# First attention without the twelve unread TensorE products that stand inside its head pairs

## The chip, the cores and the metric

The kernel runs on one core of a Trainium2 chip. The metric is the device time of one execution in microseconds; before the change the median of three runs is 1009.01 us (1003.79 to 1011.23). A core has five engines that run their own instruction streams and meet at semaphores: PE (TensorE, matrix products and transposes into PSUM), DVE (VectorE), ACT (ScalarE), POOL (GpSimd) and SP (SyncE, which here issues DMAs). TensorE's clock is granted at one of two levels, 2.4 GHz (shown as 1.00) or 1.2 GHz (0.50).

## The reference, cut to what matters

The input is `x` of 4 batch entries, 512 rows and 256 columns, in f32. Four layers follow, each with a residual and a layer norm:

- a causal softmax attention with 16 heads of 16 columns, rotary angles on the first 4 of them (the first attention);
- a gated wave layer with two levels of linear maps and norms;
- a linear attention;
- six MLP blocks with 1024 hidden columns.

```
qkv = einsum('bsh,hf->bsf', x, w_qkv) + b_qkv          # split in 16 heads, q and k rotated
scores = where(causal, einsum('bhqd,bhkd->bhqk', q, k), -inf)
attn = einsum('bhqk,bhkd->bhqd', softmax(scores), v)
x = layernorm(x + attn @ w_out + b_out)
```

The products that the change leaves out compute nothing of this: their results are never read.

## The kernel before, in words

f32 operands are split into a high and a low part (names with `_h` and `_l`), and a product is made of three.

**First attention** (function `attention0`, the four batch entries are "entries"). An entry works through 8 pairs of heads `p`, and a pair through 4 steps `r` (row tiles). In each step TensorE makes two score products (L858), two products for the row maximum of the pair two ahead (L847), a share of the value products of earlier pairs (L871), and, where a table (`WORK_AT`, `FIRST_AT`, `LAST_AT`) has an entry for the step `(p, r)`, one piece of other work (`use_work`): a projection of q, k and v (L894), a turn of the stacked heads by transposes (`turn_stack`, L901; the k half into the bank `work`, the q half into the bank `exchange`), a transpose of the next entry's `x` (`x_T`, L978), an output projection (L910), or work on later layers' weights (L935, L946, L957, L964). `work` and `exchange` are one PSUM bank each: a piece may start only when the engine that reads the piece before has counted up `work_read` or `ex_read`. An entry is "first" (entry 0), "loop" (1 and 2) or "last" (3). The order on every engine is written out by the program; nothing is reordered at run time but by these waits.

Readers: DVE finds the maxima (L1148), makes the low part of the transposed `x` (`x_l`, L1185) and adds the bias to a projection (L1197); ACT does the exponentials (L722), copies the turned heads (L709, L715), makes the high part of the transposed `x` (`x_h`, L690) and stacks heads (L701, L703); POOL masks the diagonal (L606), rotates (L591 to L595) and makes the low half of the stacks (L612, L614).

**Unread products.** `keep_busy` (L985) issues products of 128 by 128 with 512 columns of `wout_h` into a bank whose content nobody reads. It is called in three places:

- before the entries, while the second pair's maxima are made: 4, 3, 2 and 2 products (L1078);
- in `use_work` (L917 to L920), in step (0, 2) of the first entry and the two loop entries, ahead of the turn of the stack (1, 1): 3 products into `exchange` each, behind a wait until the q copy of the stack before is done;
- in `entry` (L1016 to L1019) by the table `KEEP_AT` (L316), in step (6, 2) of the first entry: 3 products into `work`, behind a wait until DVE has added the bias of the projection just made.

Ahead of the turn of a stack stand further waits: that DVE has read the transposed `x` out of `work`, and that POOL has made the stack's low half (L921, L925).

Of the kernel before, what the change touches and what calls it, by code (L numbers as in the profile page):

```python
# [194 lines left out]
def sems(stack, nc, names, of=""):  # L195
    return {n: stack.enter_context(nc.semaphore(of + n)) for n in names.split()}


def build(nc, A, out):
# [3 lines left out]
    with top:  # L203
# [109 lines left out]
BIAS_TILE_AT = ((5, 1), (5, 2), (5, 3), (6, 0))  # L313
KEEP_TILE_AT = ((6, 2), (6, 3), (7, 0), (7, 1))

KEEP_AT = {"first": {(6, 2): (3, ("project", (3, 2)))},  # L316
           "loop": {}, "last": {}}


def of_entry(when, half):  # L320
# [3 lines left out]
def work_table(when):  # L324

    table = {}
    for p, r, kind, arg in WORK_AT:
        if kind in PREVIOUS:
            used = when != "first"
        else:  # L330
            used = when != "last" if kind == "x_T" else of_entry(when, arg[0])
        if used:
            table[p, r] = (kind, arg)
    for p, r, kind, arg in {"first": FIRST_AT, "loop": (), "last": LAST_AT}[when]:
        table[p, r] = (kind, arg)
    return dict(sorted(table.items()))
# [39 lines left out]
WORK = Uses([], lambda when: list(work_table(when).values()), [])  # L376
EXCHANGE = Uses([("neg", 0)], exchange_list, [("group", -1)])


def attention0(nc, A, g, top):  # L380
# [21 lines left out]
    s = g.first = sems(top, nc, "ident_in rope_in const_in first_T first_p first_v first_s first_copied qkv_in0 qkv_in1 out_in wsplit_h wsplit_l g_wout const_v mask_v x_in xres_in g_res g_ones "  # L402
             "p_work work_read p_ex ex_read a_xT a_attT a_nT v_xT g_rope g_chain g_val a_stack stack_low "
             "p_max v_max v_neg m_row0 m_row1 p_score a_exp g_sel p_out a_out v_chain v_norm g_x1 "
             "phase_in v_turn a_sin v_mod mod_out mod_in small_in wave_rows_in path_in gate_in ent_in l1_in last_in "
             "v_bias v_matrix a_split v_split a_gate_h v_gate_l p_gate a_gate p_tail v_tail a_c")
# [29 lines left out]
    def stage_matrix(st):  # L436
        return entangled[:, MATRIX_AT[st] // 2, :, :] if MATRIX_AT[st] % 2 else raw_path[:, MATRIX_AT[st], :, :]
# [22 lines left out]
    work, outputs, exchange = ps[:, 5, :], ps[:, 6, :], ps[:, 7, :]  # L460
    block = g.block = top.enter_context(nc.Block())

    def tile_number(i, half, t):

        return RT * (2 * i + half) + t
# [17 lines left out]
    def wait(eng, sem, count):  # L483

        if not isinstance(count, int) or count > 0:
            eng.wait_ge(sem, count)
# [343 lines left out]
    def _(pe):  # L830
# [83 lines left out]

        def use_work(i, when, kind, arg):

            if (kind, arg) == ("stack", (1, 1)) and when != "last":  # L917

                pe.wait_ge(s["ex_read"], EXCHANGE.number(i, when, (kind, arg)))
                keep_busy(exchange, 3)  # L920
            wait(pe, s["work_read"], WORK.number(i, when, (kind, arg)))  # L921
            if kind == "project":
                mm = project(work, *arg)
            elif kind == "stack":
                pe.wait_ge(s["stack_low"], tile_number(i, *arg) + 1)  # L925
                mm = turn_stack(work, k_stack)
            elif kind == "out":
                mm = project_out(work, arg)
            elif kind == "bias":
                pe.wait_ge(s["small_in"], 96 + 16 * 2 * (STAGES - 1))  # L930
                mm = pe.transpose(work[:, 0:BIAS_COLS], bias_rows[:, :], ident[0:BIAS_COLS, 0:BIAS_COLS])
            elif kind == "total":
                pe.wait_ge(g.wave["v_turns"], 3)
                pe.wait_ge(s["work_read"], WORK.number(i, when, ("constant", arg)) + 1)
                mm = pe.matmul(work[:, 0:D], g.turns[:, 2:3].broadcast_to([P, P]), g.stage_c[:, 2 * arg + 1, :],  # L935
                               start=True, stop=True)
            elif kind == "constant":
                if arg:
                    pe.wait_ge(s["ent_in"], 32 * MC0)
                else:  # L940
                    pe.wait_ge(g.pre["w1_in"], 16)
                pe.wait_ge(s["v_bias"], 1)
                for m in range(MC0):
                    rows = slice(m % 4 * GROUP_ROWS, (m % 4 + 1) * GROUP_ROWS)
                    col = 4 + arg * MC0 + m
                    mm = pe.matmul(work[rows, 0:D], g.bias_col[:, col:col + 1].broadcast_to([P, GROUP_ROWS]),  # L946
                                   raw_pw[:, m, :], start=(m < 4), stop=(m >= MC0 - 4))
            elif kind == "entangle":
                l, part = arg[0], arg[-1]
                if l:  # L950
                    pe.wait_ge(s["ent_in"], 32 * MC0)
                else:
                    pe.wait_ge(g.pre["w1_in"], 16)
                    pe.wait_ge(g.pre["w2_in"], 16)
                for n in range(MC_HALF):
                    m = part * MC_HALF + n
                    mm = pe.matmul(work[:, 0:D], ent_t[:, m, arg[1] * P:(arg[1] + 1) * P], raw_pw[:, m, :],  # L957
                                   start=(n == 0), stop=(n == MC_HALF - 1))
            elif kind == "offset":

                pe.wait_ge(s["v_matrix"], MATRIX_NUMBER[arg])
                for c in range(KC):
                    col = SB_COL + (arg - 1) * KC + c
                    mm = pe.matmul(work[:, 0:D], g.bias_col[:, col:col + 1].broadcast_to([P, P]),  # L964
                                   stage_matrix(arg)[:, c, :], start=(c == 0), stop=(c == KC - 1))
            else:
                if kind == "x_T":
                    pe.wait_ge(s["x_in"], 16 * (i + 2))
                    src = x_in
                elif kind == "att_T":  # L970

                    pe.wait_ge(s["ex_read"], EXCHANGE.number(i, when, ("group", -1)) + 1)
                    src = att
                else:
                    pe.wait_ge(s["v_norm"], i + 1)
                    src = xn[:, 0, :, :]
                for t in range(RT):
                    mm = pe.transpose(work[:, t * P:(t + 1) * P], src[:, t, arg * P:(arg + 1) * P], ident[:, :])  # L978
            mm.then_inc(s["p_work"], 1)
            if kind == "stack":  # L980
                pe.wait_ge(s["ex_read"], EXCHANGE.number(i, when, (kind, arg)))
                mm = turn_stack(exchange, q_stack)
                mm.then_inc(s["p_ex"], 1)

        def keep_busy(bank, count):  # L985
            for _ in range(count):
                pe.matmul(bank, wout_h[:, 0, 0:P], wout_h[:, :, :].rearrange("p c d -> p (c d)"), start=True, stop=True)

        def entry(i, when):
            table = work_table(when)  # L990
            for p in range(PAIRS):
                for r in range(RT):
                    if (i, p, r) != (0, 0, 0):
                        score_pass(i, p, r)
                    if p + 2 < PAIRS:
                        max_pass(i, p + 2, r, (i, when))
                    elif when != "last":
                        max_pass(i + 1, p + 2 - PAIRS, r, (i, when))

                    if p % 2 and r >= 2:  # L1000
                        value_pass(i, p // 2, r - 2)
                    elif p % 2 == 0 and r < 2 and p:
                        value_pass(i, p // 2 - 1, r + 2)
                    elif p == 0 and r < 2 and when != "first":
                        value_pass(i - 1, GROUPS - 1, r + 2)
                    row_next = r == 1 and (p < PAIRS - 1 or when != "last")

                    if row_next and p != 1:
                        max_rows(i, when, p + 1, i * PAIRS + p + 1)
                    if (p, r) in table:  # L1010
                        use_work(i, when, *table[p, r])
                    if row_next and p == 1:
                        max_rows(i, when, p + 1, i * PAIRS + p + 1)
                    if group_at(p, r, when):
                        transpose_outputs(i, when, p // 2 - 1)
                    if (p, r) in KEEP_AT[when]:  # L1016
                        count, use = KEEP_AT[when][p, r]
                        wait(pe, s["work_read"], WORK.number(i, when, use))
                        keep_busy(work, count)  # L1019

        def first_project(half, t, bank):
            project(ps[:, bank, :], half, t).then_inc(s["first_p"], 1)
# [1839 lines left out]
```

## Time and profile before

| what | value |
|---|---|
| median of three runs | 1009.01 us (1003.79 to 1011.23) |
| the profiled execution: its own time | 1004.3 us |
| the profiled execution: span of the profile | 1002.3 us |
| mean granted clock of TensorE over the span | 0.996 |
| busy, share of the span: PE, DVE, ACT, POOL | 96%, 76%, 61%, 36% |

The span runs from the first to the last instruction; 2.0 us of the profiled execution's time lie around it. A busy time is the union of an engine's instructions. PE's includes the way of a product through the pipeline, so neighbouring products overlap and a fully busy PE need not be at its peak. The idle time in brackets behind a row of the timeline is the engine's, just before that row, with what ended it.

### The profile page before, as it was taken

To read this page: it belongs to the slowest core of one execution; us is meant where nothing else is said; L and a number is where in the kernel's file an instruction comes from. 1 tells how busy PE (TensorE), PEld (TensorE's weight loads), DVE (VectorE), ACT (ScalarE), POOL (GpSimd) and SP (SyncE) were. 2 spreads that over 40 slices of the span, in tenths; PEclk is the share of its full clock that TensorE was granted. 3 is DMA by queue.
4 is the path that set the end of the run, shared out by engine and by line. 5 is a ranking of instruction groups with operands and counts; after the bars stand their busy time and mean duration, and the time that the engine had idled before them with its cause. 6 is when DMAs were issued, how large, how long until landed. Compare 5 with 4: busy or idle time off the path is not lost.

```text
span 1002.3 us, 18316 instructions
## 1 busy us (share of the span) xinstructions
PE 960.4 (96%) x6487; PEld 797.8 (80%) x6487; DVE 758.4 (76%) x2090; ACT 609.2 (61%) x1177; POOL 360.6 (36%) x646
## 2 busy tenths in 40 slices
PE   8899999999899898889999999999999999999997
PEld 7565565656468897778899999999999999999897
DVE  6677787877948779867658787876878787687874
ACT  6456767656479674455546666655666655566650
POOL 4445466473221674343822222322222232222410
PEclk9899999999999999999999999999999999999999
DMA  7100011101120000022202120221212022121211
GB/s 254 32 1 23 23 33 43 43 23 55 59 54 4 1 22 23 19 88 64 84 12 63 33 64 22 64 66 31 64 31 63 23 64 67 31 62 32 63 37 50
DMA packets 55043, 47.42 MB, mean 47 GB/s; under 512 B 7108, under 2 KB 52392, under 8 KB 54952
## 3 DMA queue, kind: packets, MB, share of 16 engines
q1 hardware_dynamic: 52632, 43.75, 14.5%
q10 hardware_dynamic: 2320, 2.49, 0.8%
q8 instruction: 52, 0.85, 0.3%
q14 instruction: 39, 0.32, 0.1%
HBM read 31.40 MB, written 4.20 MB: 36 GB/s over the span
## 4 chain that ended last, share of the span: by engine, by line
PE 54%; DVE 5%; POOL 2%; issue 1%; ACT 1%; DVEq 0%; POOLq 0%; ACTq 0%
PE ps L2000 25%; PE ps L2017 24%; PE ps L1898 2%; DVE ln_stats L2418 1%; PE ps L2030 1%; PE ps L1949 1%; POOL hs L1795 1%; DVE xT_l L2552 0%; POOL x_b L1795 0%; PE ps L1912 0%; DVE amp L2454 0%; PE ps L1927 0%; DVE G_l L2558 0%; PE ps L1940 0%; PE ps L1849 0%
## 5 line engine op out<-in xcount | busy, mean ns | idle before, releaser
L2254 ACT ACTIVATE G<-ps,bias_col 128x512 f32<-128x512 f32 x192 | 135.8, 707 | 156.5 <-PE ps L2000 148.1
L2017 PE MATMUL ps<-w_l,G_h 128*128 128x256 f32 x736 | 203.8, 277 | 0.0
L2017 PE MATMUL ps<-w_h,G_l 128*128 128x256 f32 x736 | 203.8, 277 | 0.0
L2017 PE MATMUL ps<-w_h,G_h 128*128 128x256 f32 x736 | 203.7, 277 | 0.0
L2558 DVE TENSOR_TENSOR G_l<-G,G_h 128x512 fp32r<-128x512 f32 x192 | 166.3, 867 | 48.3 <-ACT G_h L2255 48.3
L1825 POOL TENSOR_TENSOR x_a<-xn,mlp_g 128x1024 f32<-128x1024 f32 x20 | 56.1, 2803 | 326.6 <-DVE xn L2584 326.6
L2000 PE MATMUL ps<-xT_h,w_h 128*128 128x512 f32 x384 | 150.3, 391 | 0.6 <-DVE xT_l L2552 0.4
L722 ACT ACTIVATE probs<-ps 128x512 f32<-128x512 f32 (+3 forms) x256 | 98.4, 441 | 85.4 <-PE ps L858 84.8
L2000 PE MATMUL ps<-xT_h,w_l 128*128 128x512 f32 x384 | 149.7, 390 | 0.0
L2000 PE MATMUL ps<-xT_l,w_h 128*128 128x512 f32 x384 | 149.5, 389 | 0.0
L2017 PEld LDWEIGHTS ps<-w_h,G_h 128*128 128x128 f32 x736 | 138.4, 188 | 0.9
L2017 PEld LDWEIGHTS ps<-w_l,G_h 128*128 128x128 f32 x736 | 138.2, 188 | 1.0
L2017 PEld LDWEIGHTS ps<-w_h,G_l 128*128 128x128 f32 x736 | 138.2, 188 | 0.0
L1148 DVE CUSTOM_DVE_ANT_0 ps<-ps,q_mask 128x128 f32<-128x128 f32 (+3 forms) x256 | 120.8, 513 | 21.0 <-PE ps L847 20.0
L2255 ACT ACTIVATE G_h<-ps,bias_col 128x512 fp32r<-128x512 f32 x192 | 135.3, 705 | 0.0
L606 POOL TENSOR_SCALAR_AFFINE_SELECT probs<-probs 128x256 f32<-128x256 f32 x128 | 52.9, 414 | 87.8 <-ACT probs L722 87.0
L2000 PEld LDWEIGHTS ps<-xT_h,w_h 128*128 128x128 f32 x384 | 72.1, 188 | 15.3 <-issue 0.6
L2000 PEld LDWEIGHTS ps<-xT_h,w_l 128*128 128x128 f32 x384 | 72.1, 188 | 15.2
L2000 PEld LDWEIGHTS ps<-xT_l,w_h 128*128 128x128 f32 x384 | 72.1, 188 | 14.0
L2572 DVE TENSOR_TENSOR rsum<-ps,x_a 128x1024 f32<-128x1024 f32 x23 | 28.2, 1225 | 68.3 <-PE ps L2017 68.3
L847 PE MATMUL ps<-heads_T 64*128 64x128 f32 (+3 forms) x256 | 56.9, 351 | 7.1 <-DVE top_score L1148 6.9
L858 PE MATMUL ps<-heads_T 64*128 64x512 f32 (+3 forms) x256 | 53.4, 413 | 2.9 <-ACT probs L722 2.2
(333 smaller groups left out, 2081.6 us busy)
## 6 DMA issues: line engine op xcount, KB each, us to landing
w_raw<-L_ffn_W_T SPq DMA_DIRECT2D x12, 1024.0 KB, 5.4
landed<-squares SPq DMA_DIRECT2D x320, 32.0 KB, 1.9
hs<-L_attn_hidden_states SPq DMA_DIRECT2D x8, 512.0 KB, 3.9
x_kept<-hs SPq DMA_DIRECT2D x4, 512.0 KB, 3.3
w_raw<-x_kept SPq DMA_DIRECT2D x2, 1024.0 KB, 5.5
out<-xn SPq DMA_DIRECT2D x3, 512.0 KB, 2.8
w_raw<-L_ffn_ent_w_T SPq DMA_DIRECT2D x1, 1024.0 KB, 9.4
w_raw<-L_ffn_ent_pw SPq DMA_DIRECT2D x1, 1024.0 KB, 11.6
```

Of the source, the lines that this page charges most:

```text
L606: pool.affine_select(diagonal, diagonal, [[0, 2], [1, P]], ALU.is_ge, 0.0, base=0, channel_multiplier=-1).then_inc(s["g_sel"], 1)
L722: act.activation(probs[:, p % 2, o, OFF[j]:OFF[j] + COLS[j]], ps[:, score_bank(r, o), 0:COLS[j]], ACT.Exp).then_inc(s["a_exp"], 1)
L847: pe.matmul(ps[:, o, 0:(t + 1) * P], heads_T[rows, p // UP, 0, p % UP, t * P:(t + 1) * P], heads_T[rows, p // UP, 1, p % UP, 0:(t + 1) * P ...
L858: pe.matmul(ps[:, score_bank(r, o), 0:COLS[j]], heads_T[rows, p // UP, 1, p % UP, j * P:(j + 1) * P], heads_T[rows, p // UP, 0, p % UP, j ...
L1148: v.tensor_tensor_reduce(ps[:, o, 0:(t + 1) * P], ps[:, o, 0:(t + 1) * P], q_mask[:, S - (t + 1) * P:S], 1.0, MASKED, ALU.add, ALU.max, to ...
L1825: pool.tensor_tensor(g.x_a[:, rows, :], xn[:, b % 2, :, :], bcast(g.mlp_g[:, i, :], 1, [P, RT, D]), ALU.mult).then_inc(feed["g_mul"], 1)
L2000: mm = pe.matmul(ps[:, hidden_bank(i, n), :], w[:, c, f * P:(f + 1) * P], x[:, b, c, :], start=(k == 0), stop=(k == 5))
L2017: mm = pe.matmul(ps[:, 4 + t // 2, (t % 2) * D:(t % 2 + 1) * D], x[b % 2][f][:, t * P:(t + 1) * P], w2_chunk(w, f), start=(k == 0), stop=( ...
L2254: act.activation(G32[n % 4], bank, ACT.Gelu, bias=bias)
L2255: act.activation(G_h[b % 2][f], bank, ACT.Gelu, bias=bias).then_inc(feed["a_g"], 1)
L2558: v.tensor_tensor(G_l[b % 2][f], G32[n % 4], G_h[b % 2][f].bitcast(F32), ALU.subtract).then_inc(feed["v_gl"], 1)
L2572: v.tensor_tensor(g.rsum[:, :, :], ps[:, 4:6, :].rearrange("p a (b c) -> p (a b) c", c=D), g.x_a[:, b * RT:(b + 1) * RT, :], ALU.add).then ...
```

## The change: the edit

The wait and the three products at the head of `use_work` go, and with them the table `KEEP_AT` and its use at the end of a step. These are 3 products in each of the first entry and the two loop entries at step (0, 2), and 3 in the first entry at step (6, 2): twelve of the 23 that `keep_busy` makes. The eleven before the entries stay.

```
-KEEP_AT = {"first": {(6, 2): (3, ("project", (3, 2)))},
-           "loop": {}, "last": {}}
...
         def use_work(i, when, kind, arg):
 
-            if (kind, arg) == ("stack", (1, 1)) and when != "last":
-
-                pe.wait_ge(s["ex_read"], EXCHANGE.number(i, when, (kind, arg)))
-                keep_busy(exchange, 3)
             wait(pe, s["work_read"], WORK.number(i, when, (kind, arg)))
...
                     if group_at(p, r, when):
                         transpose_outputs(i, when, p // 2 - 1)
-                    if (p, r) in KEEP_AT[when]:
-                        count, use = KEEP_AT[when][p, r]
-                        wait(pe, s["work_read"], WORK.number(i, when, use))
-                        keep_busy(work, count)
```

The wait that goes with the products of step (0, 2) is made again a few instructions later, ahead of the q half of the same turn (L981).

## Rows read from the trace of the kernel before

**Rows 1.** Page, busy us of the engines (share of the span) and instructions
```profile
PE 960.4 (96%) x6487; PEld 797.8 (80%) x6487; DVE 758.4 (76%) x2090; ACT 609.2 (61%) x1177; POOL 360.6 (36%) x646
```

**Rows 2.** Windows, entry 1: length, then PE, PEld, DVE, ACT, POOL busy, clock, DMA
```profile
97.17:160.23 63.06, 59.29 (x446) 37.14 (x443) 49.93 (x190) 41.57 (x106) 34.91 (x96) 1.00 0.12 36
```

**Rows 3.** Line L987, the unread products: ns min/median/max, first and last start
```profile
L987 PE MATMUL ps<-wout_h x23: 388/397/792, 24.1 to 164.8; 128*128 128x512 f32 x23
```

**Rows 4.** Timeline of PE, step (0, 2) of entries 1 and 2: start, us, work
```profile
101.15 0.96 PE L987 MATMUL ps<-wout_h 128*128 128x512 f32 x3
102.08 0.53 PE L901 MATMUL ps<-ident_r,k_stack 128*128 128x128 f32 x4
...
103.88 0.63 PE L887 MATMUL ps<-ident,out_T 128*128 128x128 f32 x4 [0.26 <-ACT heads_T L715]
105.03 0.50 PE L858 MATMUL ps<-heads_T 64*128 64x512 f32 x2 [0.53 <-ACT probs L722]
...
164.19 0.97 PE L987 MATMUL ps<-wout_h 128*128 128x512 f32 x3
165.13 0.54 PE L901 MATMUL ps<-ident_r,k_stack 128*128 128x128 f32 x4
```

**Rows 5.** Timeline of DVE, low part of the transposed x, entries 0, 1, 2
```profile
36.27 0.69 DVE L1185 TENSOR_TENSOR x_l<-ps,x_h 128x512 fp32r<-128x512 f32 x1 [0.90 <-ACT x_h L690]
...
101.33 0.69 DVE L1185 TENSOR_TENSOR x_l<-ps,x_h 128x512 fp32r<-128x512 f32 x1 [0.83 <-ACT x_h L690]
...
164.38 0.69 DVE L1185 TENSOR_TENSOR x_l<-ps,x_h 128x512 fp32r<-128x512 f32 x1 [0.83 <-ACT x_h L690]
```

**Rows 6.** Waits from 100 to 103: who for whom, us, times, longest
```profile
PEld ps L901 <- DVE x_l L1185: 0.4, 1, 0.4
```

**Rows 7.** Timeline of PE, step (6, 2) of the first entry and behind
```profile
87.31 0.98 PE L987 MATMUL ps<-wout_h 128*128 128x512 f32 x3
88.21 0.39 PE L858 MATMUL ps<-heads_T 64*128 64x256 f32 x2
...
90.33 0.32 PE L847 MATMUL ps<-heads_T 64*128 64x128 f32 x1 [0.33 <-DVE top_score L1148]
```

**Rows 8.** Timelines of ACT and DVE over the same steps
```profile
87.06 0.88 ACT L722 ACTIVATE probs<-ps 128x384 f32<-128x384 f32 x2 [1.99 <-PE ps L858]
...
88.87 0.70 DVE L1148 CUSTOM_DVE_ANT_0 ps<-ps,q_mask 128x512 f32<-128x512 f32 x1 [0.49 <-PE ps L847]
```

**Rows 9.** Timelines of PE and ACT, pair 0 of the first entry
```profile
31.40 1.03 PE L847 MATMUL ps<-heads_T 64*128 64x128 f32 x2 [0.94 <-DVE top_score L1148]
...
36.47 1.60 PE L987 MATMUL ps<-wout_h 128*128 128x512 f32 x3
37.91 0.47 PE L901 MATMUL ps<-ident_r,k_stack 128*128 128x128 f32 x4
...
39.20 1.99 PE L957 MATMUL ps<-w_raw 128*128 128x256 f32 x8
...
38.41 0.60 ACT L709 ACTIVATE heads_T<-ps 128x512 fp32r<-128x512 f32 x1 [1.28 <-PE ps L901]
```

**Rows 10.** Windows of the low clock, and of the same work in two entries
```profile
31.06:37.89 6.83, 6.32 (x26) 4.53 (x27) 4.30 (x20) 3.52 (x9) 1.64 (x4) 0.50 0.02 4
...
98.11:103.61 5.50, 5.50 (x48) 3.64 (x44) 2.93 (x12) 5.18 (x13) 2.49 (x7) 1.00 0.12 39
32.36:39.27 6.91, 6.86 (x38) 5.00 (x37) 4.23 (x14) 4.37 (x11) 1.64 (x4) 0.60 0.01 2
```

**Rows 11.** Timeline of PE, value products that only entry 1 has there
```profile
99.34 0.64 PE L871 MATMUL ps<-probs,val 128*32 128x256 f32 x8
```

**Rows 12.** Windows with idle TensorE: ahead of the low clock, and elsewhere
```profile
28.87:31.40 2.53, 1.59 (x7) 0.70 (x7) 1.43 (x6) 1.09 (x2) 0.43 (x2) 0.93 0.73 207
101.22:105.03 3.81, 3.02 (x19) 2.01 (x20) 3.24 (x10) 3.58 (x10) 1.48 (x5) 1.00 0.20 70
...
444.00:447.40 3.40, 1.78 (x12) 1.14 (x11) 3.30 (x13) 1.92 (x6) 1.48 (x2) 1.00 0.01 2
```

## The prediction

> **What bounds the kernel now.** The page comes first: TensorE is busy for 960.4 of 1002.3 us [rows 1], so time is won or lost there. The change sits in the first attention, so I cut that into entries: entry 1 takes 63.06 us, of which TensorE is busy for 59.29 and the next engine, DVE, for 49.93 [rows 2]. TensorE is the bound on average, but with 3.8 us of idle time, so an instruction less on it returns its time only where nothing else is late at that place. The line of the unread products gives their number, 23, and a median of 397 ns each [rows 3]; eleven of them stand before the entries and stay. The timelines show the twelve others as four bursts, which I call A (36.47, first entry), B (87.31, first entry), C (101.15, entry 1) and D (164.19, entry 2) [rows 4, 7, 9]. At each the question is what TensorE would do instead, and that is read from who ends the next wait. The granted clock is the second half of the question: it is at its high level all through the entries but for one stretch of 6.83 us, from 31.06 to 37.89, where it is 0.50, which is 1.2 instead of 2.4 GHz [rows 10].
>
> **C and D return nothing.** The next work is the turn of a stack, and it needs the bank that still holds the transposed `x`, until DVE has taken its low part. DVE starts that at 101.33 and takes 0.69 us, so it ends at 102.02; the turn starts at 102.08 [rows 4, 5]. At D it ends at 164.38 + 0.69 = 165.07 and the turn starts at 165.13 [rows 4, 5]. The same 0.06 us both times is how a release looks, and the weight load of the turn is indeed put down to `x_l` [rows 6]. DVE itself waits for ACT, which the products do not hold up. So the 0.96 and 0.97 us are laid over a wait that stays: 0 each, and TensorE then stands idle from about 101.22 to 102.08. What covers the edit here is DVE's wait; only if the transposed `x` came earlier would there be something to gain, at most the 0.9 us of a burst.
>
> **B returns about 0.5 us.** The products run from 87.31 to the next score product at 88.21. That one needs the first of the two exponentials that ACT makes from 87.06 in 0.88 us, so about 87.5 [rows 7, 8]: TensorE can be 0.65 us earlier. DVE stands idle for 0.49 us before the maximum that follows and is what TensorE waits for next, at 90.33 [rows 7, 8]. It can be early by those 0.49 us and not more, since before them it is at work. I take 0.5; the ends are 0 and the whole burst, 0.98.
>
> **A returns about 0.6 us.** Here the clock is low and the burst takes 1.60 us. The low part of `x` is there at 36.27 + 0.69 = 36.96, so the turn could start at 37.02 instead of 37.91: 0.89 us at most [rows 5, 9]. What follows is late for another reason: the work at 39.20 needs the bank that ACT copies from 38.41 to 39.01 [rows 9], and the turn ahead of that copy would now run at the low clock throughout. A half of it is there within 0.53 us at the high clock [rows 4] and takes longer at the low one, so I set 0.3 us against the 0.89 for both halves and take 0.6, which I chose. The ends are 0 and 0.89.
>
> The removed wait on `ex_read` costs nothing and gives nothing: it is made again ahead of the q half. No transfer, queue or operation of another engine moves; twelve weight loads go with the products.
>
> So without any effect on the clock the sum is -0.6 - 0.5 - 0 - 0 = **-1.1 us**, with ends of 0 and -0.89 - 0.98 - 0.9 - 0.9 = -3.7. The profiled execution would go from 1004.3 to 1003.2 us. It is 4.7 us under the median of the runs shown, so I carry differences over to the median: 1009.0 - 1.1 = 1007.9.
>
> **What a fall of the clock costs.** The change puts idle time into TensorE where products stood. What does the trace show of that? Ahead of the one fall TensorE was busy for 1.59 us of 2.53, with a longest gap of 0.94 us [rows 9, 12]. From 101.22 to 105.03 it is now busy for 3.02 of 3.81, and without the burst it would lose another 0.86 of that, with gaps of 0.86, 0.26 and 0.53 us [rows 4, 12]. That looks like the place of the fall. On the other side, from 444.00 to 447.40 TensorE is busy for 1.78 of 3.40 us and the clock stays at 1.00 [rows 12]. So such a gap allows a fall and does not force one, and I can only set odds: about one in three each at C and D, less at B, where the next work closes up by 0.65 of the burst's 0.98 us, and one in four at A that the clock rises later than at 37.89, since the burst fills the end of the low stretch.
>
> The price comes from the same work at both levels. From the first turn of pair 0 to the end of the maxima of step 2, entry 1 takes 5.50 us, of which 0.64 are value products that the first entry has not yet; that leaves 4.86. The first entry takes 6.91, mostly at the low clock [rows 10, 11]. So a fall costs 6.91 - 4.86 = **2.0 us**. The ends are 0, if TensorE would have waited anyway, and half of the 6.83 us, 3.4, if it did nothing but products.
>
> The Trainium skill, page "TensorE: Matmul & The Clock Gate", section "A second HAM failure mode: psum-queue depth-cycling", speaks against the change: a kernel whose TensorE idles briefly but often between groups of products can go back and forth between the two levels of the clock. By it each new gap would bring a fall. The trace agrees for the one fall at 31.06 and disagrees for 444.00 to 447.40 [rows 12], so it gets a chance and not the forecast.
>
> **The rivals.**
> Forecast: one more fall in the typical execution, from the odds above (two thirds for C and D together, about a third for A and B). -1.1 + 2.0 = +0.9, so 1009.9. Chance 0.42.
>
> No fall, only the cover is gone: 1007.9. For it speaks that the clock holds through the idle stretch at 444.00, against it that it fell once with gaps of the same length. Chance 0.28.
>
> Slower: the clock falls in the gap at the head of the entries each time, at C and D, and rises later at A. Three prices of 2.0 less the 0.5 of B: +5.5, so 1014.5. The mechanism decides where the gap ahead of the turn of stack (1, 1), the rest being the short transposes and half-height products around it, is enough by itself to bring the low level. For it speaks the match with the stretch before 31.06, against it that the trace has as idle a stretch without a fall. To be slower than 1% (10.1 us) it needs falls of 3.4 us, at which it is 3 x 3.4 - 0.5 = 9.7 and the gaps of later steps join in. Chance 0.20, of which 0.08 over 1%.
>
> Faster: the bursts are on the path after all, and the time of all four returns: 1.60 + 0.98 + 0.96 + 0.97 = 4.5 us [rows 4, 7, 9], so 1004.5. For it speaks only TensorE's busy share in entry 1; against it the equal 0.06 us at C and D. Chance 0.07.
>
> That the change does not do what it says can be all but excluded: the products have a line of their own, and 11 of 23 should be left on it. The remaining 0.03 is for a median that comes out low for no reason of the change.
>
> **How the numbers follow.** Likeliest is 1010. About 1% is what a measurement of this kernel can tell from no change, since the three runs shown lie 7.4 us apart. All cases but the far end of the slower one lie inside: within 1% 0.89, slower 0.08, faster 0.03. The range reaches from the full return, a little under 1004.5, to a little over the slower case of 1014.5: 1003.5 to 1015.
>
> **What the profile after would show.** Line L987's place has 11 products, none after 30 us. In pair 0 of entries 1 and 2 the turn starts 0.06 us after `x_l` as now, behind an idle gap of some 0.85 us put down to DVE. Behind step (6, 2) of the first entry DVE's idle time of 0.49 us is gone. The row of the granted clock tells the rest: entries 1 and 2 at 1.00 throughout mean no fall there, and a mean below 1.00 in either is one. The prediction is wrong if the turn at C or D starts well before 102.02's counterpart, if a fall costs far from 2.0 us in the same work, or if the clock is unchanged and the time yet moves by more than the bursts' 4.5 us.

## The result and the profile after

The changed kernel takes 1010.75 us in the median of 20 runs (1009.50 to 1014.73), the kernel before, beside it, 1006.30 (20 runs, 1003.41 to 1011.23). The ratio is 1.0041, 95% interval 1.0027 to 1.0054: by the ratio 4.1 us slower, within 1%. The profiled execution took 1012.74 us, 2.0 over the median; TensorE makes 6475 products in it, twelve fewer than in [rows 1].

First the clock. The windows of the changed kernel (columns as in [rows 2]) are entry 1, entry 2, and then the five stretches at the low level inside the first attention:

```profile
97.82:160.75 62.93, 58.29 (x443) 36.59 (x440) 49.88 (x190) 41.55 (x106) 34.81 (x96) 1.00 0.11 36
160.75:225.50 64.75, 60.85 (x444) 38.06 (x440) 50.04 (x190) 41.63 (x106) 34.80 (x96) 0.95 0.10 31
...
31.00:41.24 10.24, 9.24 (x40) 6.82 (x41) 6.92 (x24) 5.77 (x15) 3.33 (x9) 0.50 0.02 8
167.53:174.36 6.83, 6.71 (x37) 4.30 (x37) 4.30 (x19) 5.19 (x15) 3.55 (x11) 0.50 0.04 13
252.87:256.28 3.41, 3.41 (x20) 2.79 (x23) 3.26 (x13) 0.45 (x2) 0.66 (x2) 0.50 0.00 0
266.52:280.17 13.65, 13.50 (x42) 7.45 (x42) 10.30 (x42) 5.16 (x13) 3.11 (x6) 0.50 0.32 83
287.00:293.83 6.83, 6.20 (x32) 2.60 (x36) 2.71 (x5) 3.66 (x9) 3.90 (x8) 0.50 0.54 168
```

Where the kernel before has one low stretch of 6.83 us [rows 10], this has 41.0 us in five. The profiled execution before was one with little of it, at a mean clock of 0.996; the means over many runs, further down, lie closer together. Entry 1, which answers to [rows 2], is no longer than before (62.93 against 63.06) at a clock of 1.00: C's removal alone moved nothing.

The timeline of TensorE at C and D answers to [rows 4]; its lines are numbered lower in the changed kernel (L900 is the turn, L886 the transposes of the outputs, L846 and L857 the products for maxima and scores):

```profile
101.52 0.34 PE L846 MATMUL ps<-heads_T 64*128 64x384 f32 x2
102.72 0.54 PE L900 MATMUL ps<-ident_r,k_stack 128*128 128x128 f32 x4 [0.86 <-DVE x_l L1176]
...
104.53 0.63 PE L886 MATMUL ps<-ident,out_T 128*128 128x128 f32 x4 [0.27 <-ACT heads_T L714]
105.69 0.50 PE L857 MATMUL ps<-heads_T 64*128 64x512 f32 x2 [0.53 <-ACT probs L721]
```
```profile
165.65 0.54 PE L900 MATMUL ps<-ident_r,k_stack 128*128 128x128 f32 x4 [0.87 <-DVE x_l L1176]
...
167.46 1.04 PE L886 MATMUL ps<-ident,out_T 128*128 128x128 f32 x4 [0.27 <-ACT heads_T L714]
168.62 0.79 PE L857 MATMUL ps<-heads_T 64*128 64x512 f32 x2
```

The turn waits 0.86 us for `x_l` at C and 0.87 us at D. At C the steps then run as before; at D, with the same steps and the same gaps, the clock falls while the transposes of the outputs run, and they take 1.04 us instead of 0.63.

The low part of `x` that the turn waits for answers to [rows 5]:

```profile
101.98 0.69 DVE L1176 TENSOR_TENSOR x_l<-ps,x_h 128x512 fp32r<-128x512 f32 x1 [0.83 <-ACT x_h L689]
...
164.91 0.69 DVE L1176 TENSOR_TENSOR x_l<-ps,x_h 128x512 fp32r<-128x512 f32 x1 [0.83 <-ACT x_h L689]
```

101.98 + 0.69 = 102.67 and 164.91 + 0.69 = 165.60: the turns follow 0.05 us later.

TensorE at B, which answers to [rows 7], and at A, which answers to [rows 9]:

```profile
88.59 0.39 PE L857 MATMUL ps<-heads_T 64*128 64x256 f32 x2 [0.40 <-ACT probs L721]
89.00 0.93 PE L846 MATMUL ps<-heads_T 64*128 64x512 f32 x2
...
90.77 0.51 PE L846 MATMUL ps<-heads_T 64*128 64x128 f32 x2
```
```profile
36.98 0.75 PE L900 MATMUL ps<-ident_r,k_stack 128*128 128x128 f32 x4 [0.48 <-DVE x_l L1176]
...
39.10 3.03 PE L952 MATMUL ps<-w_raw 128*128 128x256 f32 x8
42.06 0.51 PE L857 MATMUL ps<-heads_T 64*128 64x512 f32 x2
```

At A the turn starts at 36.98 instead of 37.91, but the clock stays low until 41.24, and the eight products behind take 3.03 us where they took 1.99.

Set against the same instruction in the kernel before, the lag of the changed kernel's TensorE is +0.95 us behind A, +0.64 behind B, +0.65 behind C, +2.3 behind D, and +8.5 at the end of the attention; from there to the end of the kernel it no longer changes. The lag is the difference of the start times in the two profiles. So 6 us of the profiled execution's loss lie in the last entry, from which nothing was removed.

### The profile page after: what moved, and what is told of

Its sections match the earlier page's. It is cut to its first block, busy times and chain, and to the rows that moved or that the text cites. A ratio compares the mean times of both kernels' runs of the same rounds, so it can differ in the third digit from the quotient of the medians.

```text
span 1010.7 us, 18292 instructions
## 1 busy us (share of the span) xinstructions
PE 969.3 (96%) x6475; PEld 802.7 (79%) x6475; DVE 759.0 (75%) x2090; ACT 609.1 (60%) x1177; POOL 360.9 (36%) x646
## 4 chain that ended last, share of the span: by engine, by line
PE 54%; DVE 5%; POOL 2%; issue 1%; ACT 1%; DVEq 0%; POOLq 0%; ACTq 0%
PE ps L1991 24%; PE ps L2008 24%; PE ps L1889 2%; DVE ln_stats L2409 1%; PE ps L2021 1%; PE ps L1940 1%; POOL hs L1786 1%; DVE xT_l L2543 0%; POOL x_b L1786 0%; PE ps L1903 0%; DVE amp L2445 0%; PE ps L1918 0%; DVE G_l L2549 0%; PE ps L1931 0%; PE ps L1840 0%
## 5 line engine op out<-in xcount | busy, mean ns | idle before, releaser
L846 PE MATMUL ps<-heads_T 64*128 64x128 f32 (+3 forms) x256 | 57.7, 362 | 5.0 <-DVE top_score L1139 4.8
L857 PE MATMUL ps<-heads_T 64*128 64x512 f32 (+3 forms) x256 | 56.2, 435 | 3.1 <-ACT probs L721 2.3
## 6 DMA issues: line engine op xcount, KB each, us to landing
w_raw<-L_ffn_ent_w_T SPq DMA_DIRECT2D x1, 1024.0 KB, 10.2
```

The costliest lines, as they stand in the source:

```text
L846: pe.matmul(ps[:, o, 0:(t + 1) * P], heads_T[rows, p // UP, 0, p % UP, t * P:(t + 1) * P], heads_T[rows, p // UP, 1, p % UP, 0:(t + 1) * P ...
L857: pe.matmul(ps[:, score_bank(r, o), 0:COLS[j]], heads_T[rows, p // UP, 1, p % UP, j * P:(j + 1) * P], heads_T[rows, p // UP, 0, p % UP, j ...
```

## The experiments

Two theories stood after the result. **Theory 1**: the low stretches depend on when an idle stretch of the attention meets the clock's changes, so moving work moves them. **Theory 2**: they come at the place of the removed burst, and the last entry's are chance. The expectations were written with these names.

The table gives all runs; low time, the time at the low clock, is 2 x (1 - mean granted clock) x time, the mean over a kernel's runs. In the profiles 1.3 to 3.7 us of it lie at the end of the span, and in two of them 3.4 us near 450 us; all else lies in the attention. For the kernel before it is 18.9, 21.2 and 19.3 us in the three sets of 28 to 35 runs beside these, for the changed kernel 36.6. The changed kernel was run in the first set only; the later kernels are compared with it by their ratios and low time.

| kernel | median us (runs) | ratio to before, 95% | low time us |
|---|---|---|---|
| changed | 1010.75 (20) | 1.0041 (1.0027 to 1.0054) | 36.6 |
| before_shift10 | 1011.75 (7) | 1.0051 (1.0026 to 1.0077) | 27.2 |
| after_shift5 | 1008.80 (10) | 1.0016 (0.9997 to 1.0035) | 22.4 |
| after_last | 1008.65 (10) | 1.0020 (1.0000 to 1.0040) | 23.6 |
| before_last | 1006.67 (10) | 1.0003 (0.9982 to 1.0025) | 12.9 |
| only_A | 1010.62 (12) | 1.0032 (1.0012 to 1.0053) | 30.8 |
| only_CD | 1008.79 (12) | 1.0013 (0.9993 to 1.0033) | 25.9 |
| only_B | 1010.73 (12) | 1.0043 (1.0021 to 1.0064) | 32.4 |
| filled | 1006.51 (12) | 0.9981 (0.9961 to 1.0000) | 11.7 |
| after_filled | 1009.18 (12) | 1.0028 (1.0010 to 1.0046) | 22.9 |
| fill_early | 1005.61 (12) | 0.9977 (0.9962 to 0.9992) | 14.2 |
| fill_early_noB | 1005.52 (12) | 0.9977 (0.9955 to 0.9999) | 13.1 |
| filled2 | 1007.20 (12) | 0.9999 (0.9981 to 1.0018) | 10.9 |

**The price of low time** is read from the runs of the kernel before. In each of the three sets time follows the mean clock with a correlation of 0.98; in the last, the two fastest runs (1003.0 and 1003.1 us) have 0.997 and 0.998, the two slowest (1011.1 and 1011.3 us) 0.984. The slopes of the three sets (574, 614 and 571 us for a clock of 1) make 0.28 to 0.30 us for each us at the low clock (574 / 2 / 1007 is 0.285); 0.29 is used below. This is a mean price over all places, and a correlation: the traces show that it differs by place. The lag grows by 1.8 us over the 6.83 us at D (0.26 for each us), and in before_last's profile by 1.5 us over the 3.41 us at 145 us (0.44), where the other engines have less to do.

**before_shift10: later work, nothing removed.**

```
                         transpose_outputs(i, when, p // 2 - 1)
+                    if (i, p, r) == (2, 7, 2):
+                        pe.wait_ge(s["ex_read"], EXCHANGE.number(i, when, ("neg", PAIRS)) + 1)
+                        keep_busy(exchange, 10)
```

> The kernel before with ten more unread products at step (7, 2) of entry 2, where TensorE has no idle time: all twelve bursts stay, and everything behind is 10 x 0.21 = 2.1 us later, about as late as the changed kernel's last entry is (+2.2 us). Theory 1 (the low stretches of the last entry come from when its idle stretches fall, not from what was removed): the clock falls in the last entry as in the changed kernel's profile (three stretches there, 23.9 us in all at 0.50), so +2.1 and a further 4 to 6 us against before, ratio 1.006 to 1.008. Theory 2 (low stretches come only where a burst was taken away; the last entry's are chance): +2.1 us, ratio 1.002, with the last entry at its clock of before.

Ratio 1.0051, 5.1 us, where the ten added products make the lag grow by 2.3 in the profile (2.1 was reckoned). Most of the rest goes with low time, 27.2 us against 18.9: 8.3 x 0.29 = 2.4. Its profile has a stretch in the last entry, and two more in entries that are instruction for instruction those of the kernel before:

```profile
144.66:148.07 3.41, 3.41 (x17) 1.74 (x17) 0.74 (x5) 2.04 (x4) 0.41 (x1) 0.50 0.00 0
209.51:212.92 3.41, 3.41 (x17) 1.85 (x16) 0.61 (x4) 1.56 (x4) 0.41 (x1) 0.50 0.00 0
270.95:281.19 10.24, 10.09 (x36) 5.51 (x33) 8.64 (x35) 5.16 (x13) 3.12 (x6) 0.50 0.37 104
```

The profile of before_last has the same two. So the kernel before, which is the same program up to there, falls at 145 and 210 us too, in some executions and not in the one of [rows 10]. Theory 2's 1.002 lies outside the interval; theory 1's 1.006 to 1.008 lies above the ratio measured, its lower part still inside the interval, and its three stretches in the last entry were one, of 10.24 us.

**after_shift5: the changed kernel with more work** (the same edit on the changed kernel, with a count of 5).

> The changed kernel with five unread products at step (7, 2) of entry 2: 1.1 us more work on TensorE, none of the twelve back. Theory 1: the last entry is moved by 1.1 us to another place against the clock's changes, so its low stretches are others than the three of the changed kernel; less low time there, and the time falls below the changed kernel's although work was added (by 2 to 5 us). Theory 2: 1.1 us slower than the changed kernel, ratio to before 1.005.

Theory 1 fits and theory 2 does not: 1.1 us of added work, and 2.5 us less by the ratios (1.0041 to 1.0016); theory 2's 1.005 lies outside the interval. The two intervals overlap, but low time says the same, 22.4 us against 36.6: the ten runs have 18 to 32 us, the twenty of the changed kernel 30 to 49. In the profile the first stretch is at another place and shorter, ahead of the added work, and the last entry has one of 3.41 us:

```profile
33.75:40.58 6.83, 6.36 (x26) 4.60 (x27) 4.73 (x13) 4.45 (x13) 3.35 (x9) 0.50 0.01 2
...
286.34:289.75 3.41, 3.41 (x30) 1.22 (x26) 0.55 (x1) 1.25 (x4) 1.71 (x4) 0.50 0.46 190
```

**after_last and before_last: cover in the last entry.**

```
-           "loop": {}, "last": {}}
+           "loop": {}, "last": {(4, 1): (3, ("offset", 1)), (5, 1): (3, ("offset", 2)), (6, 0): (3, ("next_T", 0)), (6, 3): (3, ("next_T", 1)), (7, 0): (3, ("next_T", 1))}}
```

This is the edit of before_last. after_last puts the same table, with an empty "first", and its use at the end of a step into the changed kernel.

> The changed kernel with 15 unread products in idle stretches of the last entry (3 each at the end of steps (4, 1), (5, 1), (6, 0), (6, 3) and (7, 0)), none of the twelve back. If low stretches of the last entry make most of the loss (theory 1), the clock stays at 1.00 there from step (4, 1) on and 3 to 5 us come back: ratio to before 0.999 to 1.002. If the loss lies at the places of the removed bursts (theory 2), nothing comes back: ratio 1.004 or above, by up to 15 x 0.2 = 3 us of added work.

> The kernel before with the same 15 unread products in the last entry, its own 23 kept. If the last entry of the kernel before is now and then low as well (its runs lie up to 8 us apart), its median falls by 1 to 3 us and its runs lie closer together (ratio 0.997 to 0.999); if its last entry is always at 1.00, it is 0 to 3 us slower by the added work (ratio 1.000 to 1.003).

On the changed kernel half of the loss returns by the ratios (1.0020), and its ten runs have 20 to 26 us of low time, where the changed kernel's have 30 to 49. Its profile has no low stretch behind 256.19, while those at 30.91 to 41.15 and 167.44 to 174.27 are where they were:

```profile
252.78:256.19 3.41, 3.41 (x21) 2.85 (x23) 3.22 (x13) 0.45 (x2) 0.61 (x2) 0.50 0.00 0
265.00:300.00 35.00, 32.78 (x195) 19.24 (x194) 19.96 (x71) 20.66 (x46) 11.52 (x22) 1.00 0.25 80
```

On the kernel before (1.0003, and not the 0.997 to 0.999 of the first case) low time falls by 6.0 us, and the added products take back what that gives.

**only_A, only_CD, only_B: which burst matters.** The changed kernel with one kind of burst back:

```
         def use_work(i, when, kind, arg):
+            if (kind, arg) == ("stack", (1, 1)) and when == "first":
+
+                pe.wait_ge(s["ex_read"], EXCHANGE.number(i, when, (kind, arg)))
+                keep_busy(exchange, 3)
```

This is only_A; only_CD has `"loop"` in place of `"first"`, and only_B puts back the table `KEEP_AT` and its use instead.

> The changed kernel with burst A alone back (three products at step (0, 2) of the first entry). Theory 1 (time = a part without low clock, 1.2 us less than before, plus 0.29 us for each us at the low clock): A shortens the first low stretch from 10.2 to 6.8 us, 1.0 us, and costs at most the 0.6 us that its removal was to give; the low stretch near 167 us stays. So 0.4 to 1.0 us less than the changed kernel: ratio to before 1.003. Theory 2 (what matters is the place of each burst alone, and A's is the whole loss): ratio 1.000.

> The changed kernel with bursts C and D alone back (three products at step (0, 2) of both loop entries). By the prediction they cost nothing, being laid over a wait, and D keeps the clock up near 167 us, where the three profiles without it fall for 6.8 us: 2.0 us less than the changed kernel, ratio to before 1.002; mean clock 0.985 against 0.982. If the fall there had another cause, no difference to the changed kernel: 1.004.

> The changed kernel with burst B alone back (three products at step (6, 2) of the first entry). The profiles show no low stretch at B in any kernel without it, and 0.33 us given back there. So B does nothing for the clock and costs 0.3 us: mean clock 0.982 as in the changed kernel, ratio to before 1.004 to 1.005. If B kept the clock up in executions that no profile showed, the mean clock is 0.984 or more and the ratio 1.003 or less.

By the ratios C and D are worth 2.8 us of the 4.1, A 0.9 and B nothing. The three ratios are in or near what was expected (only_CD has less than its 1.002, inside the interval). Only only_B's mean clock, 0.984 where 0.982 was expected, speaks for B, and its ratio does not. The intervals of only_A and only_CD both reach into that of the changed kernel, so this rests as much on the windows of their profiles. For each of only_A, only_CD and only_B, the first stretch and the place of D (for only_B, between them, that of B):

```profile
31.21:38.04 6.83, 6.54 (x28) 4.72 (x29) 4.30 (x18) 3.52 (x9) 1.64 (x4) 0.50 0.01 2
160.00:175.00 15.00, 13.00 (x111) 8.05 (x111) 10.91 (x44) 12.15 (x31) 8.38 (x25) 1.00 0.16 54
```
```profile
31.82:42.06 10.24, 9.45 (x42) 6.98 (x42) 6.29 (x22) 5.77 (x15) 3.34 (x9) 0.50 0.01 1
...
160.00:175.00 15.00, 13.87 (x113) 8.63 (x115) 10.80 (x42) 12.26 (x32) 9.09 (x25) 1.00 0.19 54
```
```profile
31.90:42.14 10.24, 9.45 (x41) 6.93 (x41) 6.35 (x22) 5.77 (x15) 3.34 (x9) 0.50 0.01 1
84.00:94.00 10.00, 9.60 (x63) 6.14 (x55) 6.71 (x27) 4.83 (x14) 3.96 (x13) 1.00 0.00 0
168.43:175.26 6.83, 6.66 (x33) 4.45 (x37) 4.44 (x19) 5.20 (x15) 3.38 (x10) 0.50 0.07 21
```

In the kernels without other cover there, the first stretch is 6.83 us with A; without A it is 10.24 in the changed kernel, after_last, only_CD and only_B, and 6.83 in after_shift5. With D there is no low stretch near 167 us in any of eight profiles; without it there is one in five of six (only_A has none). At B none has one.

Taken together, neither theory holds alone. Low time at A and D goes with the removed burst, as theory 2 has it; that of the last entry changes where nothing was removed, as theory 1 has it.

**filled, after_filled, fill_early, fill_early_noB, filled2: cover in other gaps.** In all five, ahead of the products for the maximum, where TensorE waits for DVE (three of them write it with a table):

```
+                    if (when, p, r) == ("first", 0, 0):
+                        keep_busy(outputs, 4)
+                    elif (when, p, r) == ("loop", 5, 3):
+                        pe.wait_ge(s["ex_read"], EXCHANGE.number(i, when, ("stack", (2, 3))))
+                        keep_busy(exchange, 4)
                     if p + 2 < PAIRS:
                         max_pass(i, p + 2, r, (i, when))
```

fill_early is the kernel before with this, fill_early_noB the same without `KEEP_AT`. filled and after_filled have 14 further products in the last entry, on the kernel before and on the changed one: five and three put in the same way, and three times two at the end of the value products; filled2 has 14 there in other steps.

> The kernel before, all 23 products kept, with 26 more laid into gaps in which TensorE waits for DVE or ACT: 4 ahead of the first maxima of the first entry (gap at 30.5 to 31.4), 4 in step (5, 3) of both loop entries (gap of 0.94 us), 5 and 3 in steps (4, 2) and (5, 3) of the last entry, 2 each in steps (6, 2), (6, 3) and (7, 0). Theory 1: they cost little, since the gaps are there anyway, and the low stretches at 31, 145, 210 and in the last entry go: mean clock from 0.991 to 0.996 or more, 3 us less in the median and runs closer together; ratio 0.996 to 0.998. Theory 2 (low stretches fall by chance, or the gaps move along): ratio 1.000 to 1.003.

> The changed kernel with the same 26 products in those other gaps and none of the twelve back. Theory 1: only the low stretch near 167 us, and a later end of the first, are left; the last entry is at 1.00. Mean clock 0.990 to 0.994, time 4 to 5 us under the changed kernel, ratio to before 0.999 to 1.001, and 2 to 3 us over the kernel that has both sets. Theory 2: ratio 1.004 or above.

> The kernel before with 12 more products, laid only into the gap of 0.94 us at the start of the first entry (4) and into the gaps of 0.94 us in step (5, 3) of the loop entries (4 each). The first stretch at the low clock (6.8 us, in every profile of the kernel before) and those at 145 and 210 us (3.4 us each, in some) go: some 10 us less at the low clock, at 0.29 us for each: 2.5 to 3 us less than before, ratio 0.997 to 0.998. If the low time only moves on to the last entry, ratio 0.999 to 1.001.

> The same without burst B of the kernel before. 0.3 us less than with B, by the 0.33 us that the profiles show there: ratio 0.9965 to 0.998, not to be told from the kernel with B; if B matters for the clock, slower than that one by 1 us or more.

> The kernel before with the 12 early products and 14 in the last entry, there only in gaps in which TensorE waits for DVE: 2, 3, 4, 2 and 3 in steps (2, 3), (3, 1), (4, 2), (5, 2) and (5, 3), between the score products and the products for the maximum. If they meet the low stretches of the last entry at 246 to 275 us, the mean clock is 0.996 or more and the time 1 to 2 us under the kernel with the early products alone: ratio 0.996. If they come too late or lengthen the low stretches (a product takes twice as long there), it is as fast or slower than that one: ratio 0.998 to 1.000.

fill_early is faster than the kernel before, 0.9977 (0.9962 to 0.9992) or 2.3 us, and by the ratios than the changed kernel too. Low time falls by 5.1 us, half of the 10 that were expected, and the profile has 13.7 us in the last entry: three stretches, the first two of them shown below. Its profile shows the first low stretch gone, and the clock at 1.00 at 145 and 210 us:

```profile
28.87:39.27 10.40, 9.79 (x58) 6.59 (x58) 7.40 (x26) 6.71 (x17) 3.24 (x9) 1.00 0.15 50
140.00:150.00 10.00, 9.90 (x73) 5.92 (x72) 6.92 (x25) 4.84 (x14) 6.60 (x18) 1.00 0.06 17
205.00:215.00 10.00, 9.57 (x68) 6.20 (x69) 7.09 (x26) 5.83 (x14) 6.16 (x16) 1.00 0.09 27
248.74:252.15 3.41, 3.41 (x20) 2.69 (x22) 3.30 (x13) 0.45 (x2) 0.70 (x2) 0.50 0.02 5
262.39:269.22 6.83, 6.83 (x21) 4.42 (x21) 4.71 (x22) 3.05 (x7) 0.81 (x2) 0.50 0.27 79
```

(The profile without B keeps 3.41 us of the first stretch, from 35.13.) Behind 40 us fill_early's TensorE is 2.0 us ahead of the kernel before, of which it was 0.5 ahead at 28 us already: 1.5 us are what the 6.83 us at the low clock had cost, less the price of the four products. B makes no difference (0.9977 with and without it), as expected.

The cover in the last entry failed: filled, with 0.9981, is no faster than fill_early. In filled the five products of step (4, 2) have a wait of their own, for DVE to read the bank they write:

```profile
260.03 0.45 PE L858 MATMUL ps<-heads_T 64*128 64x384 f32 x2
262.03 2.50 PE L987 MATMUL ps<-wout_h 128*128 128x512 f32 x5 [1.55 <-DVE neg_rows L1176]
264.46 0.69 PE L847 MATMUL ps<-heads_T 64*128 64x384 f32 x2
```

TensorE stands for 1.55 us in front of the cover, where in the kernel before it stands 1.04 us without one:

```profile
263.34 0.82 PE L847 MATMUL ps<-heads_T 64*128 64x384 f32 x2 [1.04 <-DVE top_score L1148]
```

The clock falls at 261.76, and at the low level the five take 2.50 us and hold up the products for the maximum. The fall is not shown to be the cover's doing: in fill_early the clock falls in the same step without it. But over this step filled loses 3.8 us against the kernel before, and fill_early 1.1. filled2 has the least low time of all, 10.9 us (a mean clock of 0.995, where 0.996 or more was expected), and the time of the kernel before, as its second case has it: 1007.34 in the mean less 0.29 x 10.9 is 1004.2, against 1007.5 - 0.29 x 19.8 = 1001.8 for the kernel before, so its cover costs about 2.4 us. after_filled, without the twelve, falls at both C and D and stays 2.8 us over the kernel before. That is a miss: 0.999 to 1.001 was expected, with the last entry at 1.00, and the profile has 10.2 us at the low clock there; theory 2's 1.004 is inside the interval. The falls at C and D:

```profile
101.84:108.66 6.82, 6.49 (x37) 3.87 (x34) 4.25 (x21) 5.09 (x14) 3.77 (x11) 0.50 0.00 2
166.69:173.52 6.83, 6.52 (x37) 3.91 (x35) 4.26 (x21) 5.13 (x14) 3.75 (x11) 0.50 0.03 10
```

This is the one profile with a fall at C.

## Why the prediction was right, by its steps

1010.0 was forecast and 1010.75 measured. That the two times lie so close is luck: the kernel before is at 1006.30, not at the 1009.01 of the three runs shown, and as a difference +0.9 was forecast and +4.1 measured, so that two errors of some 3 us cancel. The direction and the mechanism (a gap opens, the clock falls) were those named; one term was mis-sized by more than a factor of two, and part of it lies at a place that the prediction did not name.

**C and D return nothing**: right. The turn follows `x_l` by 0.05 us, as before, and the lag against the kernel before is +0.65 on both sides of C. The idle gap is the 0.86 us that was worked out. This holds without the clock; what the removal of D costs through it is the last term.

**B returns 0.5 us**: somewhat less. 0.30 to 0.35 came back in the profiles of all seven kernels without B. TensorE stood 0.40 us for the exponential, the wait that was named.

**A returns 0.6 us**: wrong in the event. The turn came at 36.98, 0.04 from the 37.02 worked out, but the low stretch grew from 6.83 to 10.24 us and TensorE was 0.95 us behind. The odds of one in four for a later rise were too low: the stretch was 10.24 us in four of the five profiles without A and without other cover there, and in the fifth it came later as a whole.

**Without the clock, -1.1 us**: the runs agree. 1011.3 (mean) less 0.29 x 36.6 us of low time is 1000.7 for the changed kernel, against 1001.8 for the kernel before: -1.1. The exact agreement is chance: with the 0.26 that the changed kernel's own 20 runs give (a slope of 525) for both kernels, the difference is 0.6.

**A fall costs 2.0 us**: right at D. The 6.83 us near 167 cost 1.8 (the lag goes from +0.53 to +2.32), and 6.83 x 0.29 is 2.0. The price was read from a stretch of work of which, at a mean clock of 0.60 over 6.91 us [rows 10], only 5.5 us were at the low level, so part of the match is luck; and at 145 us 3.41 us cost 1.5 already.

**One fall more** is the term that was mis-sized. Low time rose by 36.6 - 19.8 = 16.8 us, which is 2.5 stretches of 6.83 us and 4.9 us, where one and 2.0 us were forecast; -1.1 + 4.9 = +3.8 is the measured 4.1 within its interval. Of the 16.8 us the profiles place about 5.7 at D (6.83 in five of six), 1.1 at C (one of six) and 2.7 at A (3.41 in four of five). So at D it was not one in three but five in six, and at C, with the same gaps, one in six.

The other 7 us are not placed by a removed burst. The runs place them in the last entry, as an estimate: cover there takes 36.6 - 23.6 = 13.0 us of low time from the changed kernel and 18.9 - 12.9 = 6.0 us from the kernel before, 7.0 more, where the scatter of the runs leaves some 5 us either way. The prediction had nothing for that entry outside its slow rival. Why it gains stays open. Lateness alone is not the reason: the last entry has 10.2 us in the profile of before_shift10, which comes to it 5.4 us later by its added products and its two earlier falls, and 13.7 us in that of fill_early, which comes to it 2.0 us earlier than the kernel before, both with all twelve bursts kept; in the profiles it has between none and 23.9 us. Nor does the sum close as well as it looks: the stretches at 145 and 210 us, 3.4 us each or one of 6.8, stand in three of the four profiles with C and D and without other cover there, and in one of five without these bursts, which would take some 3.7 us off again. One profile of each kernel is too few for more.

The rival on the slow side, falls at C and D and a later rise at A each time, was priced at 1014.5; the slowest run of the changed kernel, 1014.73, is there, the median is not. What the Trainium skill describes against the change (page "TensorE: Matmul & The Clock Gate", section "A second HAM failure mode: psum-queue depth-cycling": short idle times between groups of products can send the clock back and forth) came true in kind: without the low time the sum was -1.1 us. The profile of the changed kernel agrees at D, with gaps of 0.87 and 0.27 us ahead of the fall, and disagrees at C in the same profile, with gaps of 0.86 and 0.27 us and no fall.

## What to carry to other kernels

An unread product laid over a wait costs nothing where it stands and can be worth some 2 us through the clock (D here); so before one is taken out as waste, see which wait it covers, and look at the granted clock of several executions, not of one. Cover belongs where TensorE waits anyway, without a wait of its own: in filled, with such a wait and at the low clock, it cost more than it saved. The one gain over the kernel before lay in gaps that had no cover: four products at the start of the first entry and four in step (5, 3) of each loop entry. How much each of the two places gives was not separated; the first low stretch, there in every profile without the four, is gone in four of five with them and halved in the fifth.

## What the runs showed of the hardware

The execution, and not only the program, decides where the clock's changes meet the work. In the fourteen profiles here, whose first 20 us issue the same instructions, the trace's record of the clock has the first rise between 4.7 and 8.0 us. Where two profiles of kernels that are alike up to there have it at the same time, the stretches that follow lie at the same places: with a first rise at 4.72 and 4.71 us, before_last and before_shift10 fall at 32.03 and 32.02, 144.67 and 144.66, 209.52 and 209.51 us; with 7.11 and 7.02, the changed kernel and after_last fall at 31.00 and 30.91, 167.53 and 167.44, 252.87 and 252.78 us. The kernel before, at 7.17, has one fall where the first two have three. The spread of the kernel before, 1003 to 1011 us, goes with the mean clock (correlation 0.98), and the prediction had put it down to no cause; that the time of the first rise makes this spread is likely by these pairs and not shown for the runs.

And low time is cheaper than it looks: half the clock costs 0.29 us per us here in the mean, not 0.5. That other engines hold TensorE up as well is argued, not shown; in its favour, it costs 0.44 at 145 us, where DVE is busy for 0.60 of 3.41 us in before_last, and 0.26 at D, where DVE is busy for 4.30 of 6.83 us.
